# One chunk of edges a turn in the counting loop of a graph-network kernel, in place of a pair

## The chip, the cores and the metric

The kernel runs on one core of one Trainium2 chip. The metric is the device time of one execution in microseconds (us); a kernel's time is the median of several executions.

## The reference

Four residual graph-network layers over 1250 nodes of width 512, each ended by a layer norm. The edges (`src`, `dst`, 21250 of them, sorted by `dst`) are the same for all four, and each edge has one of two types:

```python
edge_index = jnp.stack([src, dst])
x = _layernorm(x + _L0_gnn_ref(x, edge_index, ...), axis=-1)           # one GCN layer, batch norm, gelu
x = _layernorm(x + _L1_gnn_ref(x, src, dst, ...), axis=-1)             # two GraphSAGE layers
x = _layernorm(x + _L2_gnn_ref(x, edge_index, edge_type_2, ...), axis=-1)  # two gated relational layers
x = _layernorm(x + _L3_gnn_ref(x, edge_index, ...), axis=-1)           # one GIN layer
```

Every layer sums rows of its input over the edges (`segment_sum(h[src], dst)`). The weights of the relational layers are mixtures of 30 basis matrices of 512 x 512 (`einsum('rb,bio->rio', att, basis)`).

## The kernel before, in words

The sums over edges are matrix products with a dense count matrix: for each pair of nodes and each type, the number of edges between them. The kernel first builds that matrix from the edge list (the counting stage), and then runs seven dense units ("units" 0 to 6) with it. The change is in the counting stage alone.

**Blocks and chunks.** The 1280 (padded) destination nodes are cut into 40 blocks of 32 (`NWIN`, "windows" in the code); the sorted edges lie in 170 chunks of 128. A block needs the chunks in which its edges lie. VectorE finds the first chunk and the number of chunks of each block at run time (lines 1108 to 1123) and writes them, packed, into the table `tbl`. The number is rounded up to a multiple of two there, with six at least, so that all work goes in pairs of chunks. Counted from the drawn edge list of the reference: 30 blocks touch 5 chunks, nine touch 6 (blocks 5, 11, 15, 19, 24, 25, 29, 31 and 36), and the last one, block 39, touches 2. After rounding all 40 have 6.

**One block.** TensorE and VectorE each load the block's table word into registers (`window_range`, line 440). For each chunk VectorE writes two one-hot matrices in f16: `oh_lo`, 128 x 128 (line 1130), and `oh_key`, 128 x 640 (line 1132). TensorE multiplies them, in two halves of 320 columns (line 568), and sums the chunks of a block in PSUM. The first four chunks of a block are two fixed pairs: one ahead of the loop, one behind it. What is left goes through a loop with a register bound: line 1142 on VectorE, line 578 on TensorE. Its pairs live in a ring of `MORE` = 2 slots; `s_more` counts pairs written, `s_moreu` pairs used. The fixed pairs of block w wait on VectorE until TensorE is through with block w - 2 (`s_win`), so VectorE is at most about one block ahead.

**Around it on TensorE, in a fixed order written out by hand:** the products of a block; `turn_counts` (line 589), which transposes counts of the tile of four blocks before; `degrees` (line 597) once in four blocks; and `mix` (line 612), two or three f32 products of 128 x 512 for each block, which mix the first relational layer's basis. Their inputs, 256 KB each, come by DMA from SyncE's queue (line 458) into 8 slots, and 15 of the 120 come ahead of block 0. ScalarE copies each block's counts out of PSUM (line 758). VectorE has, between blocks, `sum_counts` once in four blocks (lines 1155 and 1157) and the maxima of the input and of the first weights (lines 1262, 1265, 1193).

After block 39, ScalarE stores the last mixed group (line 771), starts the transposing DMAs (line 818), and unit 0 begins.

Of the kernel before, what the change touches and what calls it, by code (L numbers as in the profile page):

```python
# [6 lines left out]
N, D, E = 1250, 512, 21250  # L7
REL, BASES = 2, 30
P = 128
# [10 lines left out]
OH = 2 * FIXED  # L20
MORE = 2
LEAST = 3
EPS = 1e-5
# [25 lines left out]
def resnorm_gnn_kernel(nc, x, src_t, dst_t, typ_t, dst_r, W0, b0, gamma, beta,  # L49
# [11 lines left out]
    with ctx:  # L61
# [77 lines left out]

        oh_key = zview(2 * KEYS * 2 * (OH + MORE))  # L140
        oh_lo = zview(2 * P * 2 * (OH + MORE))
        iota_n = hview(2 * KEYS)
# [17 lines left out]

        zview(2 * (2 * NT * D) - (2 * (KEYS + P) * 2 * (OH + MORE) + 5 * 4 * NWIN))
        B = zview(2 * 2 * NT * REL * P).rearrange("p (j s r c) -> p j s r c", j=2, s=NT, r=REL)
# [268 lines left out]
        XS_FROM = 4  # L431
        Z_SCALED = 40

# [4 lines left out]
        def window_range(eng, w):  # L438

            word = eng.value_load(tbl[0:1, ds(w, 1)], min_val=0, max_val=(NWIN * CHUNKS // 2 << 16) - 1)  # L440
            why = "packed so, from values clamped there"
            first = nc.s_assert_within(eng.snap(word & 255), 0, CHUNKS - 2 * LEAST, skip_runtime_bounds_check_because=why)
            more = nc.s_assert_within(eng.snap((word >> 8) & 255), LEAST - FIXED, CHUNKS // 2 - FIXED, skip_runtime_bounds_check_because=why)
            return first, more, eng.snap(word >> 16)
# [117 lines left out]
        def _(pe):  # L562

            def pair_product(slot, j, start=False, stop=False):

                for q in range(2):
                    for b in range(2):
                        last = nc.tensor.matmul(Dp[:, j, b, 0:HALF], oh_lo[:, ds(slot * (2 * P) + q * P, P)],  # L568
                                                oh_key[:, ds(slot * (2 * KEYS) + (q * KEYS + b * HALF), HALF)],
                                                start=start and q == 0, stop=stop and q == 1)  # L570
                return last

            def window(w, j):
                _, more, base = window_range(pe, w)
                wait(pe, s_wev, w - 1)
                pe.wait_ge(s_oh, FIXED * w + 1)
                pair_product(FIXED * (w % 2), j, start=True)
                with pe.Fori(0, more) as i:
                    pe.wait_ge(s_more, base + i + 1)
                    pair_product(pe.snap(((base + i) & (MORE - 1)) + OH), j).then_inc(s_moreu, 1)  # L580
                pe.wait_ge(s_oh, FIXED * (w + 1))
                pair_product(FIXED * (w % 2) + 1, j, stop=True).then_inc(s_win, 1)
# [480 lines left out]
        def _(dve):  # L1063
# [45 lines left out]
            link(v.tensor_scalar(w_st, rngr[:, 0:NWIN], -1.0, 256.0, ALU.mult, ALU.add))  # L1109
            link(v.tensor_scalar(w_st, w_st, float(CHUNKS - 2 * LEAST), None, ALU.min))  # L1110
            link(v.tensor_tensor(w_n, rngr[:, NWIN:2 * NWIN], w_st, ALU.subtract))
            link(v.tensor_scalar(w_n, w_n, float(2 * LEAST), 1.0, ALU.max, ALU.add))
            link(v.tensor_scalar(w_n, w_n, 0x1FE, None, ALU.bitwise_and))
            link(v.tensor_scalar(w_p, w_n, 0.5, -float(FIXED), ALU.mult, ALU.add))
            a, step = 0, 1
# [10 lines left out]

            def pair_of(w, slot, c):

                for q in range(2):
                    v.tensor_scalar(oh_lo[:, ds(slot * (2 * P) + q * P, P)], iota_n[:, 0:P],  # L1130
                                    lo_f[:, ds(c + q, 1)], None, ALU.is_equal)
                    last = v.tensor_scalar(oh_key[:, ds(slot * (2 * KEYS) + q * KEYS, KEYS)], iota_n,  # L1132
                                           wkey[:, w:w + 1], key_f[:, ds(c + q, 1)], ALU.add, ALU.is_equal)
                return last

            def windows(w0, w1_):
                ends = "the chunks of a window end at the last chunk"
                for w in range(w0, w1_):
                    first, more, base = window_range(dve, w)
                    wait(dve, s_win, w - 1)  # L1140
                    pair_of(w, FIXED * (w % 2), first).then_inc(s_oh, 1)
                    with dve.Fori(0, more) as i:
                        c = nc.s_assert_within(dve.snap(first + i * 2 + 2 * FIXED), 0, CHUNKS - 2,
                                               skip_runtime_bounds_check_because=ends)
                        n = dve.snap(base + i)
                        dve.wait_ge(s_moreu, n + 1)
                        pair_of(w, dve.snap((n & (MORE - 1)) + OH), c).then_inc(s_more, 1)
                    pair_of(w, FIXED * (w % 2) + 1, nc.s_assert_within(dve.snap(first + 2), 0, CHUNKS - 2,
                                                                       skip_runtime_bounds_check_because=ends)).then_inc(s_oh, 1)
# [390 lines left out]
```

## Time and profile before

| | |
|---|---|
| time, median of 3 executions | 944.89 us (941.42 to 945.36) |
| time of the profiled execution | 940.41 us |
| its span | 938.4 us |
| granted TensorE clock, mean | 0.984 of full speed |
| TensorE matmuls busy | 893.2 us, 95% of the span |
| VectorE busy | 681.1 us, 73% |
| ScalarE busy | 280.8 us, 30% |
| GpSimd busy | 86.1 us, 9% |

The span is the time between the first and the last instruction of the profiled execution; the time holds 2.0 us more. A busy TensorE is not one at its peak: its matmuls are pipelined and their ends are modelled, so blocks of them are best compared by their starts.

### The profile page before, as it was taken

What the parts mean: (1) busy time and instruction counts of PE and PEld (TensorE: products, weight loads), DVE (VectorE), ACT (ScalarE), POOL (GpSimd) and SP (SyncE); (2) the same over time, 40 slices, a digit from 0 to 9 for tenths busy, and PEclk for the clock granted to TensorE, in tenths of its full rate; (3) what the DMA queues carried; (4) which work ended last, traced back from release to release, by engine and by line L of the source; (5) the groups of instructions that cost most, each with busy time, mean ns of one, the idle gap of its engine ahead of it and who ended that gap; (6) DMA issues with size and microseconds to landing.
All of it is one profiled execution on the core that took longest, in us unless ns stands there. A gap on an engine that the chain in (4) does not pass through costs nothing.

```text
span 938.4 us, 13110 instructions
## 1 busy us (share of the span) xinstructions
PE 893.2 (95%) x4320; PEld 433.9 (46%) x4320; DVE 681.1 (73%) x1469; ACT 280.8 (30%) x431; POOL 86.1 (9%) x66
## 2 busy tenths in 40 slices
PE   6798999999996999999999899999999999999997
PEld 3354555554554544434444344444444444444443
DVE  7598998866997789798999888995324245552247
ACT  0132444443863313324132211113411131032321
POOL 1000011120321001202121000001300010010000
PEclk9899999999997999999999899999999999999999
DMA  8855556559544585788643765450031014322238
GB/s 261 275 163 157 157 182 181 171 136 232 159 147 135 144 239 177 191 248 176 182 120 97 168 147 171 124 127 12 22 79 34 1 54 115 90 66 46 39 66 229
DMA packets 134779, 129.53 MB, mean 138 GB/s; under 512 B 80575, under 2 KB 81044, under 8 KB 134714
## 3 DMA queue, kind: packets, MB, share of 16 engines
q10 hardware_dynamic: 96192, 60.25, 25.2%
q1 hardware_dynamic: 38522, 68.45, 25.0%
q8 instruction: 36, 0.59, 0.3%
q14 instruction: 29, 0.24, 0.1%
HBM read 97.80 MB, written 12.52 MB: 118 GB/s over the span
## 4 chain that ended last, share of the span: by engine, by line
PE 64%; DVE 17%; DMA 7%; ACT 4%; issue 3%; DVEq 1%; ACTq 1%; POOL 1%
PE Dp L658 24%; PE Dp L688 24%; PE T L612 9%; PE Dp L568 5%; DVE acc L1239 4%; DVE Zraw L1350 1%; DMA xr<-xres 1%; DVE stt L1331 1%; ACT W L1002 1%; DMA wst<-mixd 1%; DVE w L1368 1%; ACT wst L853 1%; DMA Zraw<-in_basis 1%; DMA stage<-in_basis 1%; POOL Zraw L525 1%
## 5 line engine op out<-in xcount | busy, mean ns | idle before, releaser
L658 PE MATMUL Dp<-W,hT 128*128 128x512 f16 x792 | 175.7, 381 | 3.6 <-DMA hT<-S 3.6
L688 PE MATMUL Dp<-Zraw,A 128*128 128x512 f16 x800 | 173.0, 379 | 0.0
L1239 DVE SCALAR_TENSOR_TENSOR acc<-stage,att,acc 128x512 f32<-128x512 f32 x232 | 163.7, 770 | 3.2 <-DMA stage<-in_basis 3.1
L688 PE MATMUL Dp<-Zraw,AT 128*128 128x512 f16 x600 | 130.0, 379 | 0.0
L658 PEld LDWEIGHTS Dp<-W,hT 128*128 128x128 f16 x792 | 77.7, 98 | 96.7 <-DMA hT<-S 3.8
L688 PEld LDWEIGHTS Dp<-Zraw,A 128*128 128x128 f16 x800 | 78.3, 98 | 94.4
L1132 DVE TENSOR_SCALAR Zraw<-hT,w 128x640 f16<-128x640 f16 (+1 forms) x240 | 114.4, 476 | 0.6 <-issue 0.4
L688 PEld LDWEIGHTS Dp<-Zraw,AT 128*128 128x128 f16 x600 | 58.7, 98 | 70.8
L1130 DVE TENSOR_SCALAR Zraw<-hT,w 128x128 f16<-128x128 f16 (+1 forms) x240 | 62.6, 261 | 24.8 <-PE Dp L568 15.9
L568 PE MATMUL Dp<-Zraw 128*128 128x320 f16 (+1 forms) x480 | 73.4, 300 | 3.3 <-DVE Zraw L1132 2.8
L1368 DVE SCALAR_TENSOR_TENSOR w<-Dp,aggc,S 128x512 f32<-128x512 f32 x40 | 29.9, 747 | 60.0 <-PE Dp L688 54.0
L954 ACT ACTIVATE Zraw<-Dp,zsc 128x512 f16<-128x512 f32 x46 | 29.4, 684 | 126.3 <-PE Dp L658 122.9
L612 PE MATMUL T<-stage,W 128*128 128x512 f32 x120 | 60.4, 626 | 7.2 <-DVE W L1095 7.2
L568 PEld LDWEIGHTS Dp<-Zraw 128*128 128x128 f16 (+1 forms) x480 | 46.7, 98 | 44.2 <-issue 27.7
L612 PE MATMUL T<-Zraw,W 128*128 128x512 f32 x120 | 58.4, 609 | 6.6 <-DMA Zraw<-in_basis 6.6
L1308 DVE SCALAR_TENSOR_TENSOR Zraw<-Dp,zsc,Zraw 128x512 f16<-128x512 f32 x26 | 19.5, 749 | 59.0 <-ACT Zraw L954 59.0
L525 POOL TENSOR_TENSOR W<-wst,W 128x1024 f16<-128x1024 f32 x18 | 43.1, 2415 | 159.7 <-ACT W L856 159.7
L993 ACT ACTIVATE w<-w,s_in 128x512 f32<-128x512 f32 x30 | 21.6, 720 | 120.5 <-DVE w L1368 115.5
L758 ACT ACTIVATE Zraw<-Dp 128x640 f16<-128x640 f32 x40 | 28.1, 701 | 97.6 <-PE Dp L568 95.5
L658 PE MATMUL Dp<-W,stage 128*128 128x512 f16 x240 | 52.8, 379 | 1.2 <-DVE Zraw L1308 1.2
L713 PE MATMUL Dp<-AT,Zraw 128*128 128x512 f16 (+1 forms) x240 | 43.4, 344 | 0.0
L658 PE MATMUL Dp<-W,wst 128*128 128x512 f16 x144 | 34.0, 401 | 4.9 <-DVE S L1316 4.9
(174 smaller groups left out, 913.7 us busy)
## 6 DMA issues: line engine op xcount, KB each, us to landing
stage<-in_basis SPq DMA_DIRECT2D x180, 256.0 KB, 2.9
Zraw<-in_basis SPq DMA_DIRECT2D x60, 256.0 KB, 2.8
xres<-w ACTq DMA_DIRECT2D x30, 256.0 KB, 2.4
xr<-xres ACTq DMA_DIRECT2D x30, 256.0 KB, 2.9
wst<-in_Wn ACTq DMA_DIRECT2D x4, 1024.0 KB, 5.5
wst<-in_Ws ACTq DMA_DIRECT2D x4, 1024.0 KB, 5.6
wst<-mixd ACTq DMA_DIRECT2D x4, 1024.0 KB, 5.9
wst<-in_root ACTq DMA_DIRECT2D x3, 1024.0 KB, 6.8
```

The costliest lines, as they stand in the source:

```text
L525: pool.tensor_tensor(weights_of(u, m)[:, 1, 2 * h:2 * h + 2, :], source, weights_of(u, m)[:, 0, 2 * h:2 * h + 2, :], ALU.subtract).then_in ...
L568: last = nc.tensor.matmul(Dp[:, j, b, 0:HALF], oh_lo[:, ds(slot * (2 * P) + q * P, P)], oh_key[:, ds(slot * (2 * KEYS) + (q * KEYS + b * H ...
L612: nc.tensor.matmul(T[:, 1, :], mixT[:, b * P:(b + 1) * P], mix_in[n % MIX_SLOTS], start=(b == 0), stop=(b == PAIRS - 1)).then_inc(s_mx, 1)
L658: last = nc.tensor.matmul(dense_bank(u, t, m), turned[:, hp, k * P:(k + 1) * P], weights_of(u, m)[:, wp, k, :], start=(n == 0), stop=(n == ...
L688: last = nc.tensor.matmul(sum_bank(t), a[:, k, ds(t * P, P)], Z[:, r, h, k, :], start=(n == 0), stop=(n == count - 1))
L713: last = nc.tensor.matmul(Df[:, j, c:c + w], Z[:, 0, h, k, b * P:(b + 1) * P], AT[:, k, c:c + w], start=(k == 0 and h == 0), stop=(k == NT ...
L758: nc.scalar.activation(B[:, t % 2, :, :, a:a + WIN].rearrange("p s r (b d) -> p b (s r) d", b=2), Dp[:, w % 2, 0:2, 0:HALF].rearrange("p b ...
L954: nc.scalar.activation(Z[:, r, 0, ds(t, 1), :], dense_rows(u, t, r), ACT.Copy, scale=scale).then_inc(s_zhi[u], 1)
L1130: v.tensor_scalar(oh_lo[:, ds(slot * (2 * P) + q * P, P)], iota_n[:, 0:P], lo_f[:, ds(c + q, 1)], None, ALU.is_equal)
L1132: last = v.tensor_scalar(oh_key[:, ds(slot * (2 * KEYS) + q * KEYS, KEYS)], iota_n, wkey[:, w:w + 1], key_f[:, ds(c + q, 1)], ALU.add, ALU ...
L1239: last = v.scalar_tensor_tensor(part, stage[:, q, :], a, part, ALU.mult, ALU.add)
L1368: v.scalar_tensor_tensor(w1[:, j:j + 1, :], sum_bank(t).rearrange("p (a d) -> p a d", a=1), c, rest, ALU.mult, ALU.add).then_inc(s_pre[u], 1)
```

## The change

The loop takes one chunk each turn. `MORE` is now 4 slots of a chunk in place of 2 of a pair (the same bytes). A block has at least 5 chunks (`LEAST`), and its number is no longer rounded: the table holds the number less the four fixed chunks, 1 or 2, as the loop's bound. Three VectorE instructions of the table's making become one. The two fixed pairs stay.

```diff
-MORE = 2
-LEAST = 3
+MORE = 4
+LEAST = 2 * FIXED + 1
...
+            def chunk_product(slot, j, start=False, stop=False):
+                for b in range(2):
+                    last = nc.tensor.matmul(Dp[:, j, b, 0:HALF], oh_lo[:, ds(slot * P, P)],
+                                            oh_key[:, ds(slot * KEYS + b * HALF, HALF)], start=start, stop=stop)
                 return last
+            def pair_product(pair, j, start=False, stop=False):
+                chunk_product(2 * pair, j, start=start)
+                return chunk_product(2 * pair + 1, j, stop=stop)
...
                 with pe.Fori(0, more) as i:
                     pe.wait_ge(s_more, base + i + 1)
-                    pair_product(pe.snap(((base + i) & (MORE - 1)) + OH), j).then_inc(s_moreu, 1)
+                    chunk_product(pe.snap(((base + i) & (MORE - 1)) + 2 * OH), j).then_inc(s_moreu, 1)
...
-            link(v.tensor_scalar(w_n, w_n, float(2 * LEAST), 1.0, ALU.max, ALU.add))
-            link(v.tensor_scalar(w_n, w_n, 0x1FE, None, ALU.bitwise_and))
-            link(v.tensor_scalar(w_p, w_n, 0.5, -float(FIXED), ALU.mult, ALU.add))
+            link(v.tensor_scalar(w_p, w_n, float(LEAST), -2.0 * FIXED, ALU.max, ALU.add))
...
+            def chunk_of(w, slot, c):
+                v.tensor_scalar(oh_lo[:, ds(slot * P, P)], iota_n[:, 0:P], lo_f[:, ds(c, 1)], None, ALU.is_equal)
+                return v.tensor_scalar(oh_key[:, ds(slot * KEYS, KEYS)], iota_n,
+                                       wkey[:, w:w + 1], key_f[:, ds(c, 1)], ALU.add, ALU.is_equal)
+            def pair_of(w, pair, c):
+                chunk_of(w, 2 * pair, c)
+                return chunk_of(w, 2 * pair + 1, c + 1)
...
                     with dve.Fori(0, more) as i:
-                        c = nc.s_assert_within(dve.snap(first + i * 2 + 2 * FIXED), 0, CHUNKS - 2,
+                        c = nc.s_assert_within(dve.snap(first + i + 2 * FIXED), 0, CHUNKS - 1,
                                                skip_runtime_bounds_check_because=ends)
                         n = dve.snap(base + i)
                         dve.wait_ge(s_moreu, n + 1)
-                        pair_of(w, dve.snap((n & (MORE - 1)) + OH), c).then_inc(s_more, 1)
+                        chunk_of(w, dve.snap((n & (MORE - 1)) + 2 * OH), c).then_inc(s_more, 1)
```

## Rows read from the trace of the kernel before

**Rows 1.** The page's busy times (engine, busy us, share, instructions).
```profile
PE 893.2 (95%) x4320; PEld 433.9 (46%) x4320; DVE 681.1 (73%) x1469; ACT 280.8 (30%) x431; POOL 86.1 (9%) x66
```

**Rows 2.** The page's costliest groups, lines of the counting (busy, mean ns, idle before).
```profile
L1132 DVE TENSOR_SCALAR Zraw<-hT,w 128x640 f16<-128x640 f16 (+1 forms) x240 | 114.4, 476 | 0.6 <-issue 0.4
...
L568 PE MATMUL Dp<-Zraw 128*128 128x320 f16 (+1 forms) x480 | 73.4, 300 | 3.3 <-DVE Zraw L1132 2.8
```

**Rows 3.** Windows: stretch, its length, busy us of each engine, clock, DMA share, GB/s.
```profile
15.00:34.00 19.00, 12.36 (x35) 5.34 (x34) 9.85 (x36) 1.30 (x2) 0.00 (x0) 0.83 1.00 333
...
90.00:120.00 30.00, 29.81 (x173) 16.94 (x172) 28.60 (x97) 11.90 (x20) 2.35 (x2) 1.00 0.56 168
```

**Rows 4.** Timeline of TensorE, start of the stage (start, us, instruction, idle before).
```profile
21.71 1.79 PE L568 MATMUL Dp<-Zraw 128*128 128x320 f16 x12
...
30.14 2.05 PE L612 MATMUL T<-Zraw,W 128*128 128x512 f32 x2 [6.64 <-DMA Zraw<-in_basis]
```

**Rows 5.** The chain that ended last, end of the stage (start, us, what).
```profile
203.00 2.65 PE T L612 x6
...
205.67 0.60 ACT gw L771
```

**Rows 6.** Timeline of TensorE: the block products with idle time before or in them.
```profile
72.38 0.70 PE L568 MATMUL Dp<-Zraw 128*128 128x320 f16 x4 [1.43 <-DVE Zraw L1132]
73.72 1.51 PE L568 MATMUL Dp<-Zraw 128*128 x8 [0.63 <-DVE Zraw L1132]
...
86.71 1.53 PE L568 MATMUL Dp<-Zraw 128*128 x8 [0.55 <-DVE Zraw L1132]
...
91.16 2.33 PE L568 MATMUL Dp<-Zraw 128*128 128x320 f16 x12
...
197.25 0.72 PE L568 MATMUL Dp<-Zraw 128*128 x4 [0.20 <-issue]
```

**Rows 7.** Timeline of TensorE, one block in mid-stage, and the second after it.
```profile
100.09 1.79 PE L568 MATMUL Dp<-Zraw 128*128 128x320 f16 x12
101.72 0.39 PE L589 MATMUL Dp<-ident,Zraw 128*128 128x128 f16 x4
...
108.42 1.79 PE L568 MATMUL Dp<-Zraw 128*128 128x320 f16 x12
```

**Rows 8.** Timeline of VectorE, one block: first two chunks, and the next block's first.
```profile
104.45 0.25 DVE L1130 TENSOR_SCALAR Zraw<-hT,w 128x128 f16<-128x128 f16 x1 [0.64 <-issue]
...
104.97 0.25 DVE L1130 TENSOR_SCALAR Zraw<-hT,w 128x128 f16<-128x128 f16 x1
...
107.77 0.25 DVE L1130 TENSOR_SCALAR Zraw<-hT,w 128x128 f16<-128x128 f16 x1
```

**Rows 9.** Line 440 in 104.2 to 108.0: sequencers' table loads (ns, start us).
```profile
L440 PEldq TENSOR_LOAD <-tbl x1: 302/302/302, 104.8 to 104.8; - x1
...
L440 DVEq TENSOR_LOAD <-tbl x1: 303/303/303, 106.9 to 106.9; - x1
```

**Rows 10.** Line 1142 in the same stretch: VectorE's loop registers and branch.
```profile
L1142 DVEq FUSED_REGOPS  x2: 79/138/196, 104.9 to 106.1; - x2
...
L1142 DVEq COMPARE_BRANCH  x1: 55/55/55, 106.3 to 106.3; - x1
```

**Rows 11.** Line 578 in the same stretch: TensorE's loop branch.
```profile
L578 PEldq COMPARE_BRANCH  x1: 74/74/74, 107.7 to 107.7; - x1
```

**Rows 12.** Timeline of VectorE: one of the maxima between blocks 6 to 9.
```profile
57.23 1.21 DVE L1262 TENSOR_REDUCE xcol<-acc 128x1 f32<-128x1024 f32 x1
```

**Rows 13.** Line 1113, one instruction of the table's making.
```profile
L1113 DVE TENSOR_SCALAR Zraw<-Zraw x1: 183/183/183, 11.7 to 11.7; 128x40 int32<-128x40 int32 x1
```

**Rows 14.** Line 1142 over the whole trace: its branches.
```profile
L1142 DVEq COMPARE_BRANCH  x40: 43/43/61, 17.6 to 197.7; - x40
```

**Rows 15.** DMA queues of the page, instruction fetches; and the median landing of a basis load.
```profile
q8 instruction: 36, 0.59, 0.3%
...
stage<-in_basis SPq DMA_DIRECT2D x180, 256.0 KB, 2.9
```

More of the change, by code:

```diff
@@ L138, in resnorm_gnn_kernel @@
         hview = carver(hT[:, :, :, :].rearrange("p a h d -> p (a h d)"))
-        oh_key = zview(2 * KEYS * 2 * (OH + MORE))
-        oh_lo = zview(2 * P * 2 * (OH + MORE))
+        oh_key = zview(2 * KEYS * (2 * OH + MORE))
+        oh_lo = zview(2 * P * (2 * OH + MORE))
         iota_n = hview(2 * KEYS)
@@ L159, in resnorm_gnn_kernel @@
         w_c = [zview(4 * NWIN).bitcast(f32) for _ in range(2)]
-        zview(2 * (2 * NT * D) - (2 * (KEYS + P) * 2 * (OH + MORE) + 5 * 4 * NWIN))
+        zview(2 * (2 * NT * D) - (2 * (KEYS + P) * (2 * OH + MORE) + 5 * 4 * NWIN))
         B = zview(2 * 2 * NT * REL * P).rearrange("p (j s r c) -> p j s r c", j=2, s=NT, r=REL)
@@ L431, in resnorm_gnn_kernel @@
         XS_FROM = 4
-        Z_SCALED = 40
+        Z_SCALED = 38
         def halves_split(u):
@@ L438, in window_range @@
         def window_range(eng, w):
-            word = eng.value_load(tbl[0:1, ds(w, 1)], min_val=0, max_val=(NWIN * CHUNKS // 2 << 16) - 1)
+            word = eng.value_load(tbl[0:1, ds(w, 1)], min_val=0, max_val=(NWIN * CHUNKS << 16) - 1)
             why = "packed so, from values clamped there"
-            first = nc.s_assert_within(eng.snap(word & 255), 0, CHUNKS - 2 * LEAST, skip_runtime_bounds_check_because=why)
-            more = nc.s_assert_within(eng.snap((word >> 8) & 255), LEAST - FIXED, CHUNKS // 2 - FIXED, skip_runtime_bounds_check_because=why)
+            first = nc.s_assert_within(eng.snap(word & 255), 0, CHUNKS - LEAST, skip_runtime_bounds_check_because=why)
+            more = nc.s_assert_within(eng.snap((word >> 8) & 255), LEAST - 2 * FIXED, CHUNKS - 2 * FIXED, skip_runtime_bounds_check_because=why)
             return first, more, eng.snap(word >> 16)
@@ L562, in _ @@
         def _(pe):
[L564 to L570, printed above, removed]
-                return last
+            def chunk_product(slot, j, start=False, stop=False):
+                for b in range(2):
+                    last = nc.tensor.matmul(Dp[:, j, b, 0:HALF], oh_lo[:, ds(slot * P, P)],
+                                            oh_key[:, ds(slot * KEYS + b * HALF, HALF)], start=start, stop=stop)
+                return last
+            def pair_product(pair, j, start=False, stop=False):
+                chunk_product(2 * pair, j, start=start)
+                return chunk_product(2 * pair + 1, j, stop=stop)
             def window(w, j):
@@ L1109, in _ @@
             link(v.tensor_scalar(w_st, rngr[:, 0:NWIN], -1.0, 256.0, ALU.mult, ALU.add))
-            link(v.tensor_scalar(w_st, w_st, float(CHUNKS - 2 * LEAST), None, ALU.min))
+            link(v.tensor_scalar(w_st, w_st, float(CHUNKS - LEAST), None, ALU.min))
             link(v.tensor_tensor(w_n, rngr[:, NWIN:2 * NWIN], w_st, ALU.subtract))
-            link(v.tensor_scalar(w_n, w_n, float(2 * LEAST), 1.0, ALU.max, ALU.add))
-            link(v.tensor_scalar(w_n, w_n, 0x1FE, None, ALU.bitwise_and))
-            link(v.tensor_scalar(w_p, w_n, 0.5, -float(FIXED), ALU.mult, ALU.add))
+            link(v.tensor_scalar(w_p, w_n, float(LEAST), -2.0 * FIXED, ALU.max, ALU.add))
             a, step = 0, 1
@@ L1125, in _ @@
             dve.wait_ge(s_const, 8)
[L1127 to L1134, printed above, removed]
+            def chunk_of(w, slot, c):
[5 more added lines that the diff above has]
+                return chunk_of(w, 2 * pair + 1, c + 1)
             def windows(w0, w1_):
```

## The prediction

> **What bounds the kernel now.** I read the page first: TensorE's matmuls are busy 95% of the span, VectorE 73% [rows 1]. That is a mean over stages, so the next views are those of the counting stage, the only one that the change touches. The groups say how much of it there is: 480 matmuls of line 568 are 240 chunks, six for each of 40 blocks, so every block runs the loop once, with one pair in it [rows 2]. The windows show which engine is full. In 90 to 120 us TensorE is busy 29.81 of 30 us, but VectorE 28.60 as well [rows 3]: TensorE is the bound, VectorE comes close behind, and both must be costed. The timeline shows how TensorE's day goes: from 30.14 us, where it had waited 6.64 us for a basis matrix [rows 4], to 205.65 us, where the last mix ends [rows 5], block follows block with hardly a hole; its holes are under line 568 [rows 6]. The chain of waits goes from that last mix through ScalarE's copy of it, started 0.02 us later, into unit 0 [rows 5]. So whatever TensorE gains between 30.14 and 205.65 us moves the rest of the kernel forward, and what it gains before 30.14 us is swallowed by the wait for the DMA. Every load behind the stage is released by an event in it, and none by the clock; I know of nothing that would give the time back.
>
> **TensorE's own work.** Block by block the products take 101.72 - 100.09 = 1.63 us for 12 matmuls [rows 7], 0.136 us each by their starts, 0.272 us a chunk. By the counts of the edge list 31 blocks now take 5 chunks in place of 6 (the 30 that touch 5, and block 39), nine take 6 as before. Block 0 is one of the 31 and runs at 21.71 us, ahead of the DMA wait [rows 4], so it gives nothing. Left are 30 x 0.272 = 8.2 us. The bounds are close: 0.272 is the pitch of matmuls in an unbroken row, and the removed ones stood in such rows.
>
> **VectorE's work.** Its engine part is 0.52 us a chunk (104.45 to 104.97) and a whole block takes 107.77 - 104.45 = 3.32 us, against 6 x 0.52 = 3.12 [rows 8]: the engine is not all of it. The rest is its sequencer, which loads the table word and computes slots and columns. For one block it has the loop from 104.9 to 106.3 + 0.06 us, and the next block's load at 106.9 [rows 9, 10]. Of the loop some 0.3 us is entry (the 196 ns of registers and what stands around them), and some 0.25 the end of a turn (79 and 55 ns and what stands between), which leaves about 0.9 for two chunks, 0.45 each. So a 5-chunk block costs the sequencer 3.3 - 0.4 = 2.9 us, with 0.35 saved as I take it; a 6-chunk block now has two turns of one chunk, one more end of a turn and some registers computed twice, and costs 0.25 to 0.5 more than today; I take 0.45. The engine saves 0.52 in the one and nothing in the other. Over 40 blocks VectorE's sequencer gives 31 x 0.35 - 9 x 0.45 = 6.8 us and its engine 31 x 0.52 = 16.1 us. Against TensorE's 8.2 the sequencer's margin shrinks by 1.4 us over the whole stage, 0.04 a block, so VectorE does not become the bound in the mean. As a check: a block lasts (205.65 - 30.14) / 39 = 4.5 us on average, and VectorE needs 2.9 or 3.75 of it, plus a maximum, a sum of counts or a stall now and then.
>
> **TensorE's sequencer.** It loads the table word at 104.8 and leaves the loop at 107.7 + 0.07 us [rows 9, 11], while the products of that block begin at 108.42, right behind the mix. It is 0.65 us ahead when it is done. One turn more, 0.7 us as an estimate from VectorE's 0.45 and 0.25, comes out of a lead that starts 3.6 us before the products, so I cost it at nothing. Without that cover it would be 9 x 0.7 = 6 us at most.
>
> **The holes.** The rows hold 1.43 + 0.63 + 0.55 + 0.20 us of idle time, and one more like the last, at 198.16 us, 0.19: 3.0 us, the tails of the matmuls hide another 0.16 at each of the five, and the row of 2.33 us has 0.54 more than the 1.79 of an unbroken block: 4.3 us in all [rows 6, 7]. At four of the five VectorE is named as late. The largest, 2.4 us at block 10 (72.38), comes from the maxima that VectorE has between blocks 6 and 9, 1.21 us each [rows 12]. There the sequencer catches up during the maxima, so a block saves the engine's 0.52: 4 x 0.52 = 2.1 us, and about 0.4 from before. TensorE comes to block 10 earlier by 8 x 0.272 = 2.2 us itself, so its start gains 0.3 more, and the second hole, behind the first pair, some 0.6, because one chunk less stands between the two pairs. The holes at 86.71 and 91.16 give 0.2 and 0.5 by the same reckoning, the two at 197 us 0.3. I take 1.9 us of the 4.3. The bounds are all 4.3 gained, and 2 us of new holes where blocks of 6 chunks come and VectorE is late by its two turns.
>
> **The rest.** The table is made with two VectorE instructions less, 0.18 us each [rows 13] with some 0.08 between them: 0.5 us, before block 0, under the DMA wait of [rows 4], which covers it; without that cover it would be a gain. The ring holds the same four chunks. The semaphores are raised once a chunk in place of once a pair, on instructions that run anyway. SyncE's queue issues the basis loads as TensorE frees slots, 5% more often; the stage moves 168 GB/s there and 333 GB/s in 15 to 34 us [rows 3], so the loads keep up.
>
> **Sum.** 8.2 + 1.9 = 10 us. The profiled execution took 940.4 us and would take 930.4. It was a fast one beside the median of the runs, 944.9, and I forecast against the median: 935 us. The kernel's measurement can tell about 0.5% from no change, 4.7 us, so this would be faster, by 1.1%.
>
> **Rivals.**
> A. VectorE's sequencer decides. For it speaks that VectorE has only 1.2 us in 30 to spare [rows 3], and that every loop turn has a fixed part. Against it, that this spare is of the engine, and the sequencer runs on while the engine is held up. If the nine 6-chunk blocks each open 0.5 us on TensorE and no hole closes, the gain is 8.2 - 4.5 = 3.7: 941 us; with half of that 939.
> B. VectorE's engine decides alone, and all holes close: 8.2 + 4.3 = 12.5 us, 932 us. Against it speaks that VectorE's block takes 3.32 us and not 3.12 [rows 8].
> C. Slower: the taken branch. All 40 branches of VectorE's loop fall through now, since each loop has one turn [rows 14]; after the change the nine 6-chunk blocks jump back, once on each of the two engines, and no row shows what that costs. From below the bound is the 43 to 61 ns of a branch not taken, from above a fetch of instructions from memory, for which the nearest row is a DMA's 2.9 us to landing [rows 15]. A jump of x us adds to VectorE's 3.75 us; with some 0.6 us to spare a block, TensorE waits x - 0.6 of it, and from x = 1.7 on nine of them eat the 10 us. At 2.9 us it is 9 x 2.3 = 21 us, 956 us for the kernel. For the low end speaks that the loop's body is some ten instructions long, while 36 fetches moved 0.59 MB, 16 KB each [rows 15], so a target so near behind is most likely still there. I take 0.1 us.
> The Trainium skill (page "Runtime: NRT & Kernel Launch", section "Instruction fetch mechanics") warns that a taken branch breaks the sequential prefetch and forces a fetch if its target is outside the current window of two 16 KB pages. By that rule a jump back of ten instructions costs nothing extra unless the loop lies across a page's edge. The trace agrees on the 16 KB a fetch; what a taken jump costs it cannot show.
> D. The gain is real in the stage but given back behind it, or the count of chunks is not what I counted: 943 to 945 us. Nothing in the chain speaks for it [rows 5].
>
> **How the numbers follow.** The forecast, 932.5 to 938 us, has 0.60; A (938 to 942) 0.17; B (931 to 932.5) 0.11; C 0.06; D 0.06. Faster by over 0.5% means below 940.2 us: the forecast, B and about half of A, 0.80. Within 0.5%: the rest of A and D, 0.14. Slower: C, 0.06. The range 931 to 940.5 us leaves out C, D and part of A.
>
> **What the profile after would show.** 418 matmuls of line 568 and 209 instructions of line 1132, against 480 and 240. Blocks of 10 matmuls of 1.36 us from first start to the next product, nine with 12. 49 branches of line 1142. The last mix ends near 195.5 us against 205.65, and the distance from there to the span's end stays 732.8 us. VectorE's blocks some 2.9 us apart where nothing else stands between, 3.75 in the nine. The holes on TensorE sum to 2 to 2.5 us. Wrong it would be if holes of 0.5 us or more stood in the nine blocks with 6 chunks (A, or with 1 us and more C), or if the tail behind the stage grew (D).

## The result, and the profile after

The changed kernel takes 935.32 us, the median of 7 executions (934.43 to 937.76). The kernel before, timed beside it, takes 941.42 us, the median of 7 (940.24 to 945.36). The ratio is 0.9934, with a 95% interval of 0.9915 to 0.9952: faster, by 6.1 us. The forecast was 935 us. It landed on the time, but it was made against a median of 944.9 us for the kernel before, and over more executions that median is 941.4. The gain was to be 10 us and is 6: the landing is in part luck.

The page of the changed kernel, its busy times and the two groups of the counting (answers to [rows 1, 2]):

```profile
PE 887.2 (95%) x4258; PEld 428.2 (46%) x4258; DVE 666.7 (71%) x1405; ACT 281.2 (30%) x431; POOL 86.8 (9%) x66
...
L1131 DVE TENSOR_SCALAR Zraw<-hT,w 128x640 f16<-128x640 f16 (+1 forms) x209 | 96.1, 460 | 0.0
...
L567 PE MATMUL Dp<-Zraw 128*128 128x320 f16 (+1 forms) x418 | 65.2, 302 | 2.5 <-DVE Zraw L1131 2.3
```

209 chunks and 418 matmuls stand there against 240 and 480: the work that was to go is gone. The profiled execution took 935.1 us, its span is 933.2 against 938.4 us. Its windows (answer to [rows 3]) show VectorE with 3.9 us of 30 to spare, where it had 1.4:

```profile
15.00:34.00 19.00, 13.50 (x41) 6.06 (x40) 8.59 (x30) 1.30 (x2) 0.00 (x0) 0.91 0.99 338
90.00:120.00 30.00, 30.00 (x178) 17.30 (x176) 26.13 (x85) 13.63 (x24) 2.31 (x2) 1.00 0.58 176
```

By this row alone the change should have relieved VectorE. What it did to VectorE's sequencer doesn't show in busy time. (The forecast's rival A read the row before as 1.2 us to spare; it is 30 - 28.60 = 1.4.)

The timeline of TensorE: the end of the DMA wait, block 2, and the stretch from block 9's mix to block 11 (answers to [rows 4, 6]).

```profile
29.62 2.04 PE L615 MATMUL T<-Zraw,W 128*128 128x512 f32 x2 [5.50 <-DMA Zraw<-in_basis]
...
36.86 1.52 PE L567 MATMUL Dp<-Zraw 128*128 128x320 f16 x10
...
64.94 2.79 PE L615 MATMUL T<-Zraw,W 128*128 128x512 f32 x6
69.79 2.93 PE L567 MATMUL Dp<-Zraw 128*128 128x320 f16 x10 [2.06 <-DVE Zraw L1131]
...
73.26 3.76 PE L615 MATMUL T<-stage,W 128*128 128x512 f32 x4
76.81 1.91 PE L567 MATMUL Dp<-Zraw 128*128 128x320 f16 x12
```

And the end of the stage, by the timeline and then by the chain that ended last (answer to [rows 5]):

```profile
190.97 0.72 PE L567 MATMUL Dp<-Zraw 128*128 128x320 f16 x4 [0.27 <-DVE Zraw L1131]
...
193.80 1.52 PE L567 MATMUL Dp<-Zraw 128*128 128x320 f16 x10
195.16 0.39 PE L592 MATMUL T<-ident,Zraw 128*128 128x128 f16 x4
```

```profile
195.55 2.65 PE T L615 x6
198.19 0.02 issue
198.22 0.61 ACT gw L774
```

**Where the time came from.** I measure the stage from the start of block 2's products, the first that stand clear of the DMA wait in all profiles, to the end of the last mix.

| us | before | changed | difference |
|---|---|---|---|
| span's start to block 2 | 38.18 | 36.86 | -1.3 |
| block 2 to the end of the last mix | 167.47 | 161.34 | -6.1 |
| from there to the span's end | 732.75 | 735.00 | +2.3 |
| span | 938.4 | 933.2 | -5.2 |

The products alone should give 29 x 0.272 = 7.9 us from block 2 on, so the stage lost 1.7 us somewhere. Comparing the starts of the blocks shows where: block 9 begins 2.95 us earlier than before, block 10 2.59, block 11 only 0.53, block 15 2.77, block 20 3.43, block 30 5.34, block 39 7.19. Block 2 was already 1.32 us earlier. From block 15 to block 39 the gain grows by 4.42 us, and the 17 blocks of 5 chunks there are worth 17 x 0.272 = 4.6: the full price. From block 2 to block 15 it grows by 1.45 us, and eleven such blocks are worth 3.0, with the holes that were to close not yet counted. So the missing time is missing there.

**The sequencer.** VectorE's register instructions, those of line 440 (the table load, once in each block) in two stretches, and those of line 1145 (the loop) in the first of them. The columns are count, ns min/median/max, first and last start.

```profile
L440 DVEq TENSOR_LOAD <-tbl x2: 300/307/314, 104.0 to 108.3; - x2
...
L440 DVEq TENSOR_LOAD <-tbl x2: 305/306/306, 166.9 to 169.9; - x2
...
L1145 DVEq FUSED_REGOPS  x4: 79/132/196, 105.4 to 107.5; - x4
L1145 DVEq COMPARE_BRANCH  x2: 43/53/63, 106.4 to 107.7; - x2
```

From one load to the next is one block. A block with 5 chunks takes 3.0 us (166.9 to 169.9), one with 6 takes 4.3 us (104.0 to 108.3; forecast 3.75). The engine's rows give the first in finer figures. VectorE's timeline: the two turns of a block of 6 and its second fixed pair's first matrix, then the first matrices of a block of 5 and of the next block:

```profile
106.03 0.25 DVE L1130 TENSOR_SCALAR Zraw<-hT,w 128x128 f16 x1
...
107.29 0.26 DVE L1130 TENSOR_SCALAR Zraw<-hT,w 128x128 f16 x1 [0.62 <-issue]
...
107.88 0.25 DVE L1130 TENSOR_SCALAR Zraw<-hT,w 128x128 f16<-128x128 f16 x1
...
167.73 0.25 DVE L1130 TENSOR_SCALAR Zraw<-hT,w 128x128 f16<-128x128 f16 x1 [0.64 <-issue]
...
170.80 0.25 DVE L1130 TENSOR_SCALAR Zraw<-hT,w 128x128 f16<-128x128 f16 x1 [0.17 <-issue]
```

The block of 5 takes 170.80 - 167.73 = 3.07 us (forecast 2.9). In the block of 6 the two turns are 1.26 us apart, where two chunks of a fixed pair are 0.52 apart [rows 8], and the engine sits idle for 0.62 us of it, put down to issue: it waits for its own sequencer.

### The profile page after: what moved, and what is told of

It reads as the page before. It is cut to its first block, busy times and chain, and to the rows that moved or that the text cites. A ratio compares the mean times of both kernels' runs of the same rounds, so it can differ in the third digit from the quotient of the medians.

```text
span 933.2 us, 12906 instructions
## 1 busy us (share of the span) xinstructions
PE 887.2 (95%) x4258; PEld 428.2 (46%) x4258; DVE 666.7 (71%) x1405; ACT 281.2 (30%) x431; POOL 86.8 (9%) x66
## 4 chain that ended last, share of the span: by engine, by line
PE 65%; DVE 17%; DMA 7%; ACT 4%; issue 3%; ACTq 1%; POOL 1%; DVEq 1%
PE Dp L691 24%; PE Dp L661 23%; PE T L615 10%; PE Dp L567 5%; DVE acc L1242 4%; DMA stage<-in_basis 2%; DVE stt L1334 1%; DVE Zraw L1353 1%; ACT W L1005 1%; DMA wst<-mixd 1%; DVE w L1371 1%; ACTq L821 1%; ACT wst L856 1%; DMA xr<-xres 1%; POOL Zraw L525 1%
## 5 line engine op out<-in xcount | busy, mean ns | idle before, releaser
L691 PEld LDWEIGHTS Dp<-Zraw,A 128*128 128x128 f16 x800 | 78.3, 98 | 94.4
L1131 DVE TENSOR_SCALAR Zraw<-hT,w 128x640 f16<-128x640 f16 (+1 forms) x209 | 96.1, 460 | 0.0
L1130 DVE TENSOR_SCALAR Zraw<-hT,w 128x128 f16<-128x128 f16 (+1 forms) x209 | 56.9, 272 | 31.4 <-PE Dp L567 15.0
L615 PE MATMUL T<-stage,W 128*128 128x512 f32 x120 | 62.8, 648 | 7.1 <-DVE W L1098 7.1
L567 PE MATMUL Dp<-Zraw 128*128 128x320 f16 (+1 forms) x418 | 65.2, 302 | 2.5 <-DVE Zraw L1131 2.3
L957 ACT ACTIVATE Zraw<-Dp,zsc 128x512 f16<-128x512 f32 x46 | 29.5, 686 | 126.4 <-PE Dp L661 122.4
L567 PEld LDWEIGHTS Dp<-Zraw 128*128 128x128 f16 (+1 forms) x418 | 40.7, 99 | 41.4 <-issue 27.0
```

Source lines behind the costliest of these rows:

```text
L615: nc.tensor.matmul(T[:, 1, :], mixT[:, b * P:(b + 1) * P], mix_in[n % MIX_SLOTS], start=(b == 0), stop=(b == PAIRS - 1)).then_inc(s_mx, 1)
L691: last = nc.tensor.matmul(sum_bank(t), a[:, k, ds(t * P, P)], Z[:, r, h, k, :], start=(n == 0), stop=(n == count - 1))
L957: nc.scalar.activation(Z[:, r, 0, ds(t, 1), :], dense_rows(u, t, r), ACT.Copy, scale=scale).then_inc(s_zhi[u], 1)
L1130: v.tensor_scalar(oh_lo[:, ds(slot * P, P)], iota_n[:, 0:P], lo_f[:, ds(c, 1)], None, ALU.is_equal)
L1131: return v.tensor_scalar(oh_key[:, ds(slot * KEYS, KEYS)], iota_n, wkey[:, w:w + 1], key_f[:, ds(c, 1)], ALU.add, ALU.is_equal)
```

## The experiments

Ten runs in three groups. All ratios are to the kernel before, run beside them on the same chip. At the start two theories stood for the missing 1.7 us. Theory M: VectorE's maxima and its sequencer set the pace up to block 15, so that what TensorE's products give back turns into waiting. Theory K: the clock. The hole at block 10 leaves TensorE idle for 2.06 us, the granted clock behind it is 0.50, the 1.2 GHz level, and everything up to block 11 takes twice as long; that ate the gain.

### The changed kernel once more

No edit.

> The changed kernel once more, nothing altered. Two things of its first profile are looked at again. (1) TensorE's clock was granted at 0.50 in 72 to 77 us, behind the hole of 2.06 us at block 10: if the hole causes it, it comes again at the same place. (2) The part behind the stage (from the end of the last mix to the end of the span) took 735.0 us there against 732.8 us before: if the change causes it, it is again 2 us longer than in a profile of the kernel before taken beside it; if it is scatter between executions, it is not.

Measured: 937.83 us (10 executions) against 942.77, ratio 0.9945 (0.9922 to 0.9969); stage 161.4 us. The windows of the two profiles of the same kernel, 72 to 77 us, the first of its first profile and the second of this one (the granted clock is the third number from the end):

```profile
72.00:77.00 5.00, 5.00 (x22) 2.48 (x21) 4.14 (x15) 1.19 (x2) 0.00 (x0) 0.50 0.13 28
```

```profile
72.00:77.00 5.00, 5.00 (x35) 3.15 (x34) 4.14 (x16) 1.19 (x2) 0.00 (x0) 0.83 0.26 71
```

In the second the clock returned sooner, and block 11 began at 75.35 instead of 76.81 us. Yet block 15 ended at 94.43 us there and at 94.47 in the first. What the clock cost was absorbed within four blocks. The part behind the stage took 734.2 us, 1.4 more than before the change.

### Keeping TensorE busy through the hole

```diff
                 mix(mix_share(w))
+                if w == 9:
+                    for _ in range(18):
+                        nc.tensor.matmul(Dp[:, 1, 2, D // 2:D], ident[:, :], iota_n[:, 0:D // 2], start=True, stop=True)
```

> The changed kernel with 18 matmuls of 256 columns more on TensorE, whose result nobody reads, issued behind the mix of block 9, where TensorE is idle for 2.1 us. Theory T (VectorE's sequencer sets the pace up to block 15): the granted clock stays at 1.00 and block 10 and 11 run faster, but TensorE then waits for VectorE at blocks 11, 13 and 15 and the kernel gains at most 0.5 us on the changed one. Theory K (the fall of the clock behind the hole eats the missing gain): 2.0 to 2.3 us faster than the changed kernel.

Measured: 937.89 us (8 executions), ratio 0.9942 (0.9918 to 0.9965); stage 161.6 us. The timeline of TensorE and the window behind it:

```profile
72.65 2.13 PE L634 MATMUL Dp<-hT,ident 128*128 128x256 f16 x18
...
76.57 0.72 PE L567 MATMUL Dp<-Zraw 128*128 128x320 f16 x4 [0.32 <-DVE Zraw L1134]
...
88.52 0.70 PE L567 MATMUL Dp<-Zraw 128*128 128x320 f16 x4 [0.70 <-DVE Zraw L1134]
```

```profile
72.00:77.00 5.00, 4.35 (x30) 2.59 (x29) 4.11 (x14) 0.00 (x0) 0.85 (x1) 1.00 0.49 157
```

The clock stayed at 1.00 in that stretch and the time did not move: the stage is as long, and the saved time stands as waits for VectorE's one-hot matrices. (This profile's DMA wait ended at 33.80 us, so its blocks stand about 5 us later in the trace.) Theory K falls.

### The weights' maximum later

```diff
-            reduce_weights(0)
             for t in range(NT):
...
+                if t == 5:
+                    reduce_weights(0)
...
-            weight_work("counts", 0, 0)
             windows_to(13)
...
+            windows_to(27)
+            weight_work("counts", 0, 0)
+            windows_to(31)
             scales(0)
```

> The changed kernel with the maximum of the first weights (line 1196, 2.27 us on VectorE) moved from ahead of block 10 to behind block 26, with its reduction over partitions and the scales behind it moved accordingly (behind block 30). By then VectorE waits for TensorE at times, so it has room. Theory T: VectorE's blocks 10 to 15 start 2.3 us sooner, the hole at block 10 closes, and the kernel is 2.3 to 3 us faster than the changed one. Theory K: the same hole closes and the clock stays up, so 2 us at least too; the two are told apart by the run with the filler. A third, that TensorE's order of work alone is the bound there, would give nothing.

Measured: 935.03 us (6 executions), ratio 0.9913 (0.9884 to 0.9943), 2.8 us less than the changed kernel in the same group. Theory M's 2.3 to 3 us seem to be met, but the stage, where the edit acts, takes 160.4 us, 1.0 less, and the medians of the unaltered changed kernel alone lie 2.5 us apart (935.32 and 937.83). Block 15 ended at 91.00 us in place of 94.4, so 3.5 us came free there, as theory M has it. But by the end of the last mix 2.8 of them were lost, most of it where the work was put; the timeline of TensorE at block 31:

```profile
160.60 0.72 PE L568 MATMUL Dp<-Zraw 128*128 128x320 f16 x4 [1.20 <-DVE Zraw L1132]
```

### A second turn in all blocks

```diff
-LEAST = 2 * FIXED + 1
+LEAST = 2 * FIXED + 2
```

Each block has at least six chunks, as in the kernel before, but takes the last two in two turns. The products are those of the kernel before; the loop is that of the changed one.

> The changed kernel, but with at least 6 chunks for each block (LEAST = 6), so that all 40 blocks do the work of before, in two turns of one chunk in place of one turn of a pair. It shows the price of the turns alone. Theory T: a 6-chunk block costs VectorE's sequencer 4.3 us as in the profile of the changed kernel, against 3.3 us for a block of before, so VectorE becomes the bound almost everywhere: 40 x 4.3 us and 20 us of other work on VectorE against a stage of 176 us, that is 12 to 25 us slower than the changed kernel. If turns are free: only the 30 chunks of TensorE come back, 8 us slower than the changed kernel, no more than 2 us from the kernel before.

Measured: 967.65 us (6 executions), ratio 1.0273 (1.0242 to 1.0305); stage 190.9 us. That is 29.8 us above the changed kernel, more than the 12 to 25 that were expected. The sequencer's table loads (count, ns, first and last start) and TensorE's timeline:

```profile
L440 DVEq TENSOR_LOAD <-tbl x2: 306/308/311, 106.1 to 110.8; - x2
```

```profile
106.89 0.72 PE L567 MATMUL Dp<-Zraw 128*128 128x320 f16 x4 [0.19 <-DVE Zraw L1131]
...
214.87 1.98 PE L567 MATMUL Dp<-Zraw 128*128 x6 [2.85 <-DVE Zraw L1131]
```

These two loads, one block, stand 4.7 us apart; where nothing else stands between, it is 4.3. Of the stage's 28 holes 22 wait for VectorE, 14.2 us of 16.4. 190.9 us over 38 blocks is 5.0 us each, where the kernel before has 167.5 / 38 = 4.4: with the same products, taking the last pair as two turns makes VectorE the bound and costs 23 us. Not all of it is the turns' own work: the largest hole, 2.85 us in block 37, stands behind two matrices that VectorE wrote while GpSimd worked (see the last section). The run says what would happen on an edge list whose blocks all touch six chunks.

VectorE's engine was busy for only 22.58 us of 30 where it was the bound (windows of this run, 90 to 120 us):

```profile
90.00:120.00 30.00, 27.50 (x149) 14.49 (x148) 22.58 (x80) 9.03 (x16) 0.00 (x0) 1.00 0.50 146
```

### The maxima earlier, on both kernels

The first four maxima of the input stand one each ahead of blocks 6 to 9, the fifth and the weights' maximum behind block 9. Here all stand behind block 2, and the weights' maximum behind block 3. The timeline of VectorE of the changed kernel shows the place, a wait for TensorE, which itself waits for the basis:

```profile
34.67 0.25 DVE L1130 TENSOR_SCALAR Zraw<-hT,w 128x128 f16<-128x128 f16 x1 [7.43 <-PE Dp L567]
```

```diff
+            windows_to(3)
+            dve.wait_ge(e_x, 48)
+            for piece in range(4):
+                v.tensor_reduce(xcol[:, piece:piece + 1], ...).then_inc(s_xc, 1)
+            v.tensor_reduce(xcol[:, 4:5], ...).then_inc(s_xc, 1)
+            dve.wait_ge(s_xc, 5)
+            v.tensor_reduce(xin[:, :], xcol[:, :], AX.X, ALU.max).then_inc(s_xin, 1)
             windows_to(4)
...
-            windows_to(6)
-            dve.wait_ge(e_x, 48)
-            for piece in range(4):
-                v.tensor_reduce(xcol[:, piece:piece + 1], ...).then_inc(s_xc, 1)
-                windows_to(7 + piece)
-            v.tensor_reduce(xcol[:, 4:5], ...).then_inc(s_xc, 1)
-            dve.wait_ge(s_xc, 5)
-            v.tensor_reduce(xin[:, :], xcol[:, :], AX.X, ALU.max).then_inc(s_xin, 1)
             weight_work("counts", 0, 0)
```

On the changed kernel:

> The changed kernel with VectorE's maxima moved out of blocks 6 to 10: the five of the input (1.13 us each) go behind block 2, where VectorE waits 7 us for TensorE and the input has landed, and that of the first weights (2.27 us) behind block 3. Theory T (between block 6 and 15 VectorE sets the pace, and so swallows part of what TensorE saves): TensorE's row from block 9 to 16 takes 34.2 us in the changed kernel and needs 28.3 us of its own work, so the kernel is 5 to 6 us faster than the changed one, near 931 us. If the stage were TensorE's alone, holes apart, the gain would be the 3.4 us of the two holes at block 10 at most.

Measured: 933.43 us (8 executions), ratio 0.9905 (0.9873 to 0.9937); stage 157.3 us, 4.0 less than before the move: less than the 5 to 6 us that theory T gave, and hardly more than the 3.4 of its rival. On the kernel before:

> The kernel before with the same move of the maxima. Theory T: it loses its holes of 4.3 us and is 4 to 4.5 us faster than the kernel before; so with the maxima out of the way the change is worth 7.5 to 8.2 us (this against the run with early maxima of the changed kernel), and not the 6 it is worth with them in the way. If the change's turns cost TensorE something by themselves, the distance of the two stays at 6 or less.

Measured: 939.81 us (12 executions), ratio 0.9973 (0.9951 to 0.9994); stage 163.3 us, 4.2 less, as expected; of the 4 to 4.5 us that were expected of the kernel's time the medians show 2.7, and in this run's profile the part behind the stage was 4 us longer. The hole at block 10 is gone in both. The five maxima now take the place of that wait (timeline of VectorE, changed kernel with early maxima):

```profile
28.88 4.60 DVE L1261 TENSOR_REDUCE xcol<-acc 128x1 f32<-128x1024 f32 x4 [0.96 <-DMA xr<-in_x]
33.39 1.21 DVE L1263 TENSOR_REDUCE xcol<-xr 128x1 f32<-128x1024 f32 x1
...
35.49 0.25 DVE L1130 TENSOR_SCALAR Zraw<-hT,w 128x128 f16<-128x128 f16 x1 [0.70 <-PE Dp L567]
```

With the maxima out of the way the change is worth 163.3 - 157.3 = 6.0 us in the stage and 939.81 - 933.43 = 6.4 in the medians: not the 7.5 to 8.2 of theory T, but the 6 of its rival. With the maxima in the way it was 6.1 in the stage. So the maxima cost each kernel some 4 us and decide where the holes stand, but none of the missing 1.7 us is theirs: that half of theory M falls, and the sequencer's half is left. What is left in the timeline is small waits; the timeline of TensorE of the changed kernel with early maxima, at block 10 (no hole) and then inside blocks 13 and 15:

```profile
68.94 1.52 PE L567 MATMUL Dp<-Zraw 128*128 128x320 f16 x10
...
81.62 0.72 PE L567 MATMUL Dp<-Zraw 128*128 128x320 f16 x4 [0.23 <-DVE Zraw L1131]
...
90.45 0.72 PE L567 MATMUL Dp<-Zraw 128*128 128x320 f16 x4 [0.22 <-DVE Zraw L1131]
```

Taken by the starts of the blocks' matmuls, they add up to 2.5 us over blocks 5, 6, 13 to 15, 19 and 38. In the kernel before with the same move block 38 alone is left, with 0.8 us by the same measure, so the difference is the missing 1.7 again. Of the other six, four are a block with a second turn or the one right behind it (5 and 6, 15, 19), and two follow one within three blocks (13 and 14, behind 11).

### The sixth chunk left out

```diff
-            link(v.tensor_scalar(w_p, w_n, float(LEAST), -2.0 * FIXED, ALU.max, ALU.add))
+            link(v.tensor_scalar(w_n, w_n, float(LEAST), float(LEAST), ALU.max, ALU.min))
+            link(v.tensor_scalar(w_p, w_n, -2.0 * FIXED, None, ALU.add))
```

All blocks take 5 chunks; the edges in the sixth chunk of nine blocks are not counted. No loop has a second turn.

> The changed kernel with exactly 5 chunks for every block: the sixth chunk of nine blocks is left out (so their counts are incomplete) and no loop has a second turn or a taken branch. TensorE's own work falls by 9 x 0.27 = 2.4 us. Theory T: VectorE is freed of two second turns of 1.25 us at blocks 11 and 15, in the stretch where it sets the pace, and behind block 15 the six others are worth TensorE's 0.27 each: 2.5 + 1.6 = 4 us faster than the changed kernel. If a second turn costs VectorE no more than a chunk's 0.5 us: 2.4 us faster or a little more.

Measured: 931.70 us (6 executions), ratio 0.9872 (0.9835 to 0.9909); stage 156.1 us against 161.3. The nine left-out chunks are 9 x 0.272 = 2.4 us of products; the other 2.8 us are holes that closed. That is above the 4 us of theory T. The second turns cost more in waits than in matmuls, although the maxima stand where they stood. The largest part lies at block 9, behind the second turn of block 5: it takes 5.64 us from start to start in place of 6.66.

### The kernel before once more

No edit.

> The kernel before, unaltered, for a second profile: how far the end of the DMA wait at block 1 (30.1 us in the first profile) and the part behind the stage (732.8 us) scatter from one execution to the next. If the 2.2 us by which the part behind the stage was longer after the change are scatter, this profile or that of the unaltered changed kernel lies outside of its own first by as much.

Measured: 940.53 us, span 938.7; stage 167.5 us, 733.1 us behind it. The stage's length repeats within 0.1 us. The part behind it is 732.75 and 733.1 us in the two profiles of this kernel, so the 2.2 us are not this kernel's scatter. Behind its hole at block 10 the clock fell too in this profile, which it did not in the first (see the last section), and block 11 came 1.4 us later, yet the stage took as long: one more sign against theory K.

### The scales later as well

On top of the early maxima, the scaling of the first weights goes behind block 24:

```diff
             v.nop().then_inc(s_s0, 1)
+            windows_to(25)
             scales(0)
```

> The changed kernel with early maxima, and besides with the scales of the first weights (1 us of small instructions on VectorE, needed only by block 35) moved from behind block 12 to behind block 24. In the profile with early maxima TensorE waits 0.4 us in block 13, 0.1 in 14 and 0.4 in 15. Theory T: VectorE's blocks 13 to 19 start 1 us sooner, these small holes close, and the stage from the end of the DMA wait to the last mix takes 0.8 to 1 us less than with early maxima alone (164.7 us), near 163.8. If the holes come from the turns of the 6-chunk blocks alone and not from what stands before them, they stay. The median can hardly tell 1 us; the profile decides.

Measured: 935.38 us (9 executions), ratio 0.9916 (0.9883 to 0.9949); stage 157.5 us. The timeline of TensorE: block 15, now without a hole as block 13 is too, and blocks 25 and 26 with new ones:

```profile
89.14 1.79 PE L567 MATMUL Dp<-Zraw 128*128 128x320 f16 x12
...
131.28 0.72 PE L567 MATMUL Dp<-Zraw 128*128 128x320 f16 x4 [0.22 <-DVE Zraw L1131]
...
136.70 0.72 PE L567 MATMUL Dp<-Zraw 128*128 128x320 f16 x4 [0.81 <-DVE Zraw L1131]
```

From the end of the DMA wait to the last mix it takes 166.2 us, where 163.8 were expected. The small holes did close, so what stood ahead of those blocks had a part in them. But the waits moved with the work: nothing was gained. It is the second move that ends so, after the one behind block 26.

### The early maxima once more

The changed kernel with early maxima, unaltered.

> The changed kernel with early maxima once more, unaltered, on the same chip as the run with the later scales: 4 to 5 us faster than the changed kernel was, a ratio of 0.989 to 0.991 to the kernel before, and again 164.7 us from the end of the DMA wait to the last mix, within 0.3.

Measured: 929.96 us (4 executions), ratio 0.9862 (0.9819 to 0.9906); stage 157.3 us. The stage repeats within 0.1 us. The stretch from the end of the DMA wait does not: it takes 165.8 us, outside of the 164.7 within 0.3 that was expected, because block 1 took 0.9 us longer. The ratio is better than expected too, and its median lies 5.4 us below that of the run with the later scales, of which the stage holds 0.2; no run shows where the rest comes from. Of the versions that compute everything, this one is the fastest in both groups that it ran in: 933.43 and 929.96 us, where the kernel before took 942.54 and 941.46.

## Why the prediction came out as it did

**TensorE's own work: right.** 480 - 418 matmuls, blocks of 10 that take 1.36 us from first start to what follows (193.80 to 195.16), and 0.27 us for each such block wherever nothing else decided, which is from block 16 on.

**TensorE's sequencer and the table: as forecast.** The two holes of the changed kernel's timeline wait for VectorE's matrices [2.06 and 0.27 us], neither for TensorE's own sequencer, and the shorter making of the table shows nowhere behind the DMA wait.

**The holes: wrong, and this is the step that failed.** The forecast said "I take 1.9 us of the 4.3", so 2 to 2.5 us of holes would be left. From block 2 on the stage gave 6.1 to 6.2 us where the products give 7.9, so holes and slow stretches grew from 4.3 to about 6.0 us. The term was +1.9 and measured -1.7. It is why the last mix ends at 198.20 us and not at 195.5: these 3.6 us are missing, less 1.0 us that came ahead of block 2 from an earlier end of the DMA wait and shorter mixes behind it, which no step had counted.

The runs split the 3.6 us in two. With the sixth chunk left out no loop has a second turn, and the stage is 167.5 - 156.1 = 11.4 us shorter than before; 38 blocks with a chunk less are 38 x 0.272 = 10.3 of it. So blocks with one turn close 1.0 us of holes, and not 1.9. The second turns then open 2.8 us, where the term had allowed for none (2 us were its worst bound). Together this is -1.8, and the stage measured -1.7.

The argument for the term was VectorE's schedule up to block 15, and its prices were too low: 3.07 us for a block of 5 chunks (forecast 2.9) and 4.3 us for one of 6 (forecast 3.75). With these, VectorE's sequencer saves 31 x 0.25 - 9 x 1.0 = -1.3 us over the stage in place of the 6.8 forecast (its block took 3.32 before [rows 8]). From block 6 to block 15 its one-hot matrices took 46.15 us before and take 44.52 now, 1.6 less for eight chunks less and two second turns more; the chunks alone are 4.2 at the engine's 0.52 us. The maxima in that stretch are no part of the error: moving them away took 4.0 us from the changed kernel and 4.2 from the one before. Giving the other 31 blocks a second turn costs 190.9 - 161.4 = 29.5 us, of which only 8 are the products.

**Rival A** (VectorE's sequencer decides) was right in its mechanism, as far as the runs with and without second turns can show it, and wrong in its place and size. It was to open 0.5 us at all nine blocks of 6 chunks. In the timeline of the changed kernel no block of 6 has a hole; the two holes stand in blocks 10 and 38 (69.79 and 190.97). The cost shows where VectorE has little lead, up to block 15 and at 19.

**Rival C** (the taken branch): its bound from above is excluded. VectorE's and TensorE's branches over the whole trace of the changed kernel, with ns min/median/max:

```profile
L1145 DVEq COMPARE_BRANCH  x49: 43/43/80, 17.1 to 190.0; - x49
...
L581 PEldq COMPARE_BRANCH  x49: 67/74/367, 23.3 to 193.3; - x49
```

49 of each, as forecast, against 40 [rows 14]. In the block above the taken branch took 63 ns on VectorE, the one not taken 43. On TensorE the taken ones took 229 to 253 ns and one of them 367, under a lead that hides it. The jump itself is cheap, near the forecast's 0.1 us on VectorE. What costs is the rest of the turn, where slot, column and semaphore value are computed from registers again. These are the register instructions of that block's second turn (lines 1130 and 1145):

```profile
L1130 DVEq FUSED_REGOPS  x2: 64/124/185, 107.0 to 107.2; - x2
...
L1145 DVEq FUSED_REGOPS  x2: 79/132/186, 106.6 to 107.5; - x2
```

A turn of one chunk comes to some 1.25 us (4.3 - 3.07, and 1.26 by the engine's rows above), where the forecast had 0.85. By the rule of the Trainium skill that was weighed there (page "Runtime: NRT & Kernel Launch", section "Instruction fetch mechanics"), a fetch is forced only where the target lies outside the current window of two pages; the trace agrees in that no branch took over 80 ns on VectorE or 367 on TensorE, far from the 2.9 us of a landing [rows 15]. The page "Advanced Engine Details and Errata", section "Control Flow Timing", of the Trainium skill gives about 108 ns for compare-and-branch, with no distinction; the trace has 43 to 80 ns on VectorE and 67 to 367 ns on TensorE, and the trace decides.

**The part behind the stage: wrong by 1 to 2 us, and only in part placed.** The forecast said 732.8 us unchanged, and knew of nothing that would give the time back. The changed kernel shows 735.0 and 734.2, the kernel before 732.75 and 733.1. A first part follows the new loop. TensorE's first wait behind the stage, for the transposing DMAs, in the kernel before and in the changed one:

```profile
213.06 2.76 PE L658 MATMUL T<-W,Zraw 128*128 128x512 f16 x12 [0.44 <-DMA Zraw<-S]
```

```profile
207.78 2.76 PE L661 MATMUL T<-W,Zraw 128*128 128x512 f16 x12 [2.60 <-DMA Zraw<-S]
```

In the three profiles with the old loop this wait is 0.4 to 0.6 us, in the nine with the new one 1.3 to 2.6 us. Some 40 us behind the last mix 1.5 us of it are left in the first profile of the changed kernel and 0.3 in the second. So rival D, the gain given back behind the stage, held in a small part. Why these DMAs land later no run shows. The rest scatters: the variants have 733.4 to 736.0 us, 735.6 and 733.4 in two profiles of one kernel, and the kernel before with early maxima has 736.9 with the short wait. Some 409 us before the span's end the changed kernel and the one before lie level again, so all of it arises in the first dense units.

**The base.** The 10 us were subtracted from a median of three executions that happened to lie high. It was 3.5 us too high and the gain 3.9 us too large. (In the profiled executions the gain is 5.3 us: the 10.1 of the sum, less 3.6 for the holes, plus 1.0 ahead of block 2, less 2.3 behind the stage, within 0.1.) The two errors cancelled, and the forecast of 935 us came out closer than its argument deserved.

## What to carry to other kernels

Price a loop with a register bound by its turns, not by its work: here the sixth chunk of a block cost 0.27 us on TensorE and 1.25 us on VectorE's sequencer, so halving what a turn does pays only where few loops take a second turn. Price the sequencer from one table load to the next, since neither the engine's busy time nor its share in a window shows it. And when a hole closes or work is moved, look for the next place where the same engine is late: twice here the waits moved along, and only the stretch under a DMA wait could really take the work.

## What was not expected of the hardware

After the 2.06 us in which TensorE had been idle, its granted clock fell to 0.50, the 1.2 GHz level. The four f32 matmuls of the mix at 73.26 us then took 3.76 us, where four of them took 1.88 to 1.96 elsewhere. It cost the kernel nothing, since VectorE set the pace for the next four blocks. Such a fall need not come: the kernel before has holes of 1.43 and 0.63 us in its first profile and of 1.44 and 0.63 in its second, and these are the windows of the two behind them:

```profile
75.00:80.00 5.00, 5.00 (x38) 3.09 (x37) 4.94 (x20) 2.02 (x4) 0.00 (x0) 1.00 0.41 95
```

```profile
75.00:80.00 5.00, 5.00 (x29) 2.92 (x28) 4.95 (x19) 1.19 (x2) 0.00 (x0) 0.70 0.18 46
```

VectorE's one-hot matrices take 0.25 and 0.45 us, but in the kernel before 12 of them took 1.1 to 2.3 us, and in the changed one 10 took 0.6 to 2.1. Each of these ran beside one of the 12 elementwise instructions that GpSimd has in the stage (lines 525 and 542, 1.2 or 2.1 us each). The run with a second turn in all blocks, block 37:

```profile
210.12 2.18 DVE L1130 TENSOR_SCALAR Zraw<-hT,w 128x128 f16 x1
210.12 4.20 POOL L525 TENSOR_TENSOR W<-wst,W 128x1024 f16<-128x1024 f32 x2 [1.87 <-ACT W L859]
212.22 2.29 DVE L1131 TENSOR_SCALAR Zraw<-hT,w 128x640 f16 x1
```

In time this reads as GpSimd holding VectorE up; no run takes GpSimd's work away, so that is argued and not shown. VectorE mostly has the lead to hide it. The 0.7 us that block 38 loses in every other profile, old loop or new, stand right behind the last two of these, as the 2.85 us hole of this run does. The forecast gave none of it a price.

Two profiles of one kernel differ in the end of the DMA wait ahead of the stage (28.3 to 33.8 us over the profiles taken here). The last in this row is that of the kernel with filler matmuls, whose stage was as long as any:

```profile
33.80 2.05 PE L615 MATMUL T<-Zraw,W 128*128 128x512 f32 x2 [10.03 <-DMA Zraw<-in_basis]
```

That wait, 5.5 us in one profile and 10.0 in another, can account for much of the scatter between executions, though only profiled ones show it, and it is why the stage's own length was the better measure for edits worth a few microseconds.
